# Predicting a reordering of row statistics, scatters, softmax sums and gate rows in an adaLN transformer block

## The reference

```python
mod = (silu(c) @ wmod).reshape(B, 6, 1, -1)
sa, ca, ga, sb, cb, gb = mod[:, 0], ..., mod[:, 5]
h = layernorm(x) * (1 + ca) + sa
x = x + ga * attention(h)          # probs = softmax(causal scores), out = probs @ v @ w_o
h = layernorm(x) * (1 + cb) + sb
x = x + gb * moe(h)                # tok/slot tables, 16 experts, scatter-add, plus shared expert
```

## Time and profile before

| | |
|---|---|
| runs, median (lowest to highest) | 1308.64 us (1308.13 to 1310.06) |
| the profiled execution | 1310.89 us, span 1309.1 us |
| mean granted TensorE clock | 0.95 |
| busy: TensorE matmul / weight load | 87% / 67% |
| busy: VectorE / ScalarE / GpSimd | 65% / 48% / 34% |
| moved by DMA | 114.36 MB, mean 87 GB/s |

### The profile page before, as it was taken

One profiled execution on the slowest core, in us unless ns is written; L12 is line 12 of the kernel. 1 busy time (PEld: TensorE's weight loads), 2 busy tenths in 40 slices (PEclk: granted clock), 3 DMA queues, 4 the chain that ended last, 5 costly groups with the idle time before them and its releaser, 6 DMA issues.

```text
span 1309.1 us, 23512 instructions
## 1 busy us (share of the span) xinstructions
PE 1141.5 (87%) x6444; PEld 882.1 (67%) x6444; DVE 848.4 (65%) x2468; ACT 633.2 (48%) x1840; POOL 439.4 (34%) x460
## 2 busy tenths in 40 slices
PE   6459999998999899998999899998999899998793
PEld 4347777776677677676677677676677677776462
DVE  3447857784687657774688657773788658774641
ACT  2237634565256544564256544564256544663120
POOL 1112104441344305340344305350334315441454
PEclk8779999998999899998999899998999899999897
DMA  9554203530153203530153203530153203430693
GB/s 307 145 129 105 70 1 81 146 84 13 32 145 81 64 1 83 143 93 5 36 145 78 64 1 89 137 97 1 43 144 78 59 0 98 119 91 2 193 255 38
DMA packets 87436, 114.36 MB, mean 87 GB/s; under 512 B 16226, under 2 KB 50976, under 8 KB 87336
## 3 DMA queue, kind: packets, MB, share of 16 engines
q1 hardware_dynamic: 68296, 98.55, 29.2%
q0 software_dynamic: 7168, 6.20, 2.4%
q10 hardware_dynamic: 11872, 8.65, 2.4%
HBM read 35.56 MB, written 15.11 MB: 39 GB/s over the span
## 4 chain that ended last, share of the span: by engine, by line
PE 51%; DVE 17%; issue 11%; DMA 6%; SPq 5%; ACT 4%; POOL 3%; ACTq 2%; DVEq 1%; POOLq 0%
PE PS L780 7%; PE PS L738 5%; PE PS L740 5%; PE PS L739 5%; PE PS L759 4%; SPq L444 4%; PE PS L909 3%; DMA qT<-qstage 3%; PE PS L938 3%; DVE qr L1350 2%; PE PS L888 2%; PE PS L890 2%; DVE pT L1381 2%; PE PS L708 2%; ACT probs L1111 2%
## 5 line engine op out<-in xcount | busy, mean ns | idle before, releaser
L1111 ACT ACTIVATE probs<-probs,nmax 128x512 f32<-128x512 f32 (+3 forms) x512 | 283.2, 554 | 214.5 <-DVE nmax L1364 212.3
L1364 DVE CUSTOM_DVE_ANT_0 probs<-PS,cmask 128x512 f32<-128x512 f32 (+3 forms) x512 | 231.4, 489 | 148.3 <-PE PS L740 121.1
L738 PE MATMUL PS<-kTh,qT 128*128 128x512 f32 (+3 forms) x512 | 182.6, 357 | 62.8 <-DMA qT<-qstage 25.8
L739 PE MATMUL PS<-kTl,qT 128*128 128x512 f32 (+3 forms) x512 | 169.4, 331 | 0.0
L740 PE MATMUL PS<-kTh,qT 128*128 128x512 f32 (+3 forms) x512 | 168.7, 329 | 0.0
L547 POOL TENSOR_TENSOR qr<-qr 128x512 f32<-128x512 f32 x64 | 81.2, 1269 | 257.0 <-DVE qr L1350 256.8
L759 PE MATMUL PS<-ident,probs 128*128 128x128 f32 x1280 | 160.0, 279 | 0.3 <-ACT pT L1120 0.3
L1120 ACT ACTIVATE pT<-PS 128x384 f32<-128x384 f32 (+3 forms) x320 | 125.4, 455 | 69.7 <-PE PS L759 69.2
L780 PE MATMUL PS<-pT,kmat 128*64 128x512 f32 (+3 forms) x1024 | 158.3, 452 | 0.3 <-issue 0.3
L738 PEld LDWEIGHTS PS<-kTh,qT 128*128 128x128 f32 x512 | 99.9, 195 | 86.0 <-issue 32.0
L759 PEld LDWEIGHTS PS<-ident,probs 128*128 128x128 f32 x1280 | 143.6, 143 | 11.6 <-issue 7.7
(11 more groups left out here) (254 smaller groups left out, 1855.7 us busy)
## 6 DMA issues: line engine op xcount, KB each, us to landing
qT<-qstage SPq DMA_DIRECT2D x128, 256.0 KB
qT<-qstage SPq DMA_DIRECT2D x256, 128.0 KB
x_in<-in_x SPq DMA_DIRECT2D x8, 512.0 KB, 6.4
modb<-mod_dram SPq DMA_DIRECT2D x8, 512.0 KB, 6.1
h_dram<-mod_dram SPq DMA_DIRECT2D x1, 4096.0 KB
h_dram<-h SPq DMA_DIRECT2D x8, 512.0 KB, 3.4
out<-base SPq DMA_DIRECT2D x8, 512.0 KB, 4.3
pT<-in_wo SPq DMA_DIRECT2D x1, 2048.0 KB, 11.0
```

Of the source, the lines that this page charges most:

```text
L738: pe.matmul(PS[:, bank, 0:n], qh, kTh[:, 0:n], start=True, stop=False)
L739: pe.matmul(PS[:, bank, 0:n], qh, kTl[:, 0:n], start=False, stop=False)
L1111: act.activation(probs[:, UO[u]:UO[u] + UW[u]], probs[:, UO[u]:UO[u] + UW[u]], ACT.Exp, scale=-1.0, bias=nmax[:, u:u + 1], accum_out=psums ...
L1364: dve.tensor_tensor_reduce(out=probs[:, UO[u]:UO[u] + UW[u]], in0=PS[:, SBANK[u], 0:UW[u]], in1=cmask[:, S - UW[u]:S], scale=-1.0, scalar= ...
```

## The change

Five things are moved.

1. `h1_statistics` is cut in two: bn_stats of tiles 0 and 1 at the end of step 4, of tiles 2 and 3 with all bn_aggr at the end of step 5. `h1_normed` stands in step 6 where the statistics stood.
2. GpSimd's scatters: rounds of three in steps 1 to 4, of four in step 5, none in step 6. The root for h1 is cut out of `roots_pre` and stands behind the last scatter; the wait for the scatters' landing comes after it.
3. `invert_sums` keeps the reciprocal; the spreading copy is GpSimd's (`widen`), between its addition and its subtraction of the query two steps ahead, and alone in steps 6 and 7.
4. `q_low` on VectorE comes behind both `group_out` copies in all steps.
5. The gate rows are written by batch, 512 rows at a time: those of batch 0 after the first three queries, those of batch n after `load_modb(n)`.

Besides, TensorE's latent projection of query 0 in the middle now comes ahead of the wait for h2.

```diff
-            sp.dma_start(h2_dram[0:T, H:].rearrange("(b s) h -> b s h", s=S),
-                         mod_dram[:, 3 * H:].unsqueeze(1).to_broadcast([B, S, H])).then_inc(gates_out, 16)
+            def gate_rows(b):
+                sp.dma_start(h2_dram[bass.ts(b, S), H:].unsqueeze(0),
+                             mod_dram[bass.ds(b, 1), 3 * H:].unsqueeze(1).to_broadcast([1, S, H])).then_inc(gates_out, 16)
...
                 store_batch(b)
                 load_modb(n)
+                gate_rows(n)
...
+            def widen(g):
+                wait_alone(pool, inv_ready, g + 1)
+                pool.tensor_copy(wide[:].rearrange("p (t h d) -> p h t d", t=NT, h=2),
+                                 prec[:].rearrange("p (h t) -> p h t", h=2).unsqueeze(3).to_broadcast(
+                                     [P, 2, NT, KL])).then_inc(wide_ready, 1)
...
-                for j in range(3 * (p - 1), min(3 * p, NT * TOPK)):
+                for j in range(3 * (p - 1), 3 * p if p < NPAIR - 3 else NT * TOPK):
...
                 if pre:
                     pe.wait_ge(kql_ready, 3 * (n + 1))
                     q_rotary(0, n * NPAIR, not post)
+                if pre:
+                    q_latent(0, n * NPAIR, not post)
                 if post:
                     pe.wait_ge(n2_ready, 2 * b + 1)
                     turn_h2()
-                if pre:
-                    q_latent(0, n * NPAIR, not post)
...
                 dve.wait_ge(exp_ready, g * NU + NU)
-                ch.step(dve.reciprocal(prec[:], psums[:]))
-                dve.tensor_copy(wide[:].rearrange("p (t h d) -> p h t d", t=NT, h=2),
-                                prec[:].rearrange("p (h t) -> p h t", h=2).unsqueeze(3).to_broadcast(
-                                    [P, 2, NT, KL])).then_inc(wide_ready, 1)
+                dve.reciprocal(prec[:], psums[:]).then_inc(inv_ready, 1)
...
                 if p == NPAIR - 2 and more:
                     modulation(b + 1)
-                    h1_statistics(b + 1)
+                    h1_normed(b + 1)
...
                 invert_sums(g)
-                if rope and not first:
-                    q_low(g + 2)
                 if not first:
                     values_out(p - 1, g - 1)
                 elif more:
                     gated(b - 1, 1)
                 group_out(g, 3)
-                if rope and first:
+                group_out(g, 5)
+                if rope:
                     q_low(g + 2)
-                group_out(g, 5)
+                if more and p in (NPAIR - 4, NPAIR - 3):
+                    h1_statistics(b + 1, p - NPAIR + 4)
                 if not last:
                     maxima(g + 1, (0, 1, 2))
```

More of the change, by code:

```diff
@@ L52 @@
 HALF = DR // 2
-CHAIN_PROLOGUE, CHAIN_BATCH = 30, 60
+CHAIN_PROLOGUE, CHAIN_BATCH = 29, 52
 MOVES = 6
@@ L311, in adaln_block @@
         exp_ready = sem("exp_ready")
+        inv_ready = sem("inv_ready")
         wide_ready = sem("wide_ready")
@@ L464, in _ @@
             sp.dma_start(h2_dram[T:T + P, H:], zrow[:]).then_inc(gates_out, 16)
-            sp.dma_start(h2_dram[0:T, H:].rearrange("(b s) h -> b s h", s=S),
-                         mod_dram[:, 3 * H:].unsqueeze(1).to_broadcast([B, S, H])).then_inc(gates_out, 16)
+            def gate_rows(b):
+                sp.dma_start(h2_dram[bass.ts(b, S), H:].unsqueeze(0),
+                             mod_dram[bass.ds(b, 1), 3 * H:].unsqueeze(1).to_broadcast([1, S, H])).then_inc(gates_out, 16)
             for p in range(3):
                 move_query(0, p, p < 2)
+            gate_rows(0)
             with sp.Fori(0, B - 1) as b:
@@ L527, in root, with root_h1, roots_kv @@
                 pool.tensor_tensor(dst, dst, mhalf[:, 0:dst.shape[1]], ALU.pow).then_inc(ready, 1)
-            def roots_pre(n):
+            def root_h1(n):
                 wait_alone(pool, var1_ready, NT * (n + 1))
                 root(rstd[:], mv[:, :, 1], LN_EPS, eps1, rs1_ready, n)
+            def roots_kv(n):
                 wait_alone(pool, ssq_ready, 8 * (n + 1))
@@ L542, in roots_post, with query_rotary @@
                 root(rstd2[:, 3:], mv2[:, 3:, 1], LN_EPS, eps2, rs2_ready, 2 * b + 1)
-            def query_rotary(g):
+            def widen(g):
[3 more added lines that the diff above has]
+                                     [P, 2, NT, KL])).then_inc(wide_ready, 1)
+            def query_rotary(g, w=None):
                 wait_alone(pool, turned_ready, g + 1)
                 pool.tensor_tensor(qr[:, 0, :], qr[:, 0, :], qr[:, 1, :], ALU.add).then_inc(rope_ready, 1)
+                if w is not None:
+                    widen(w)
                 wait_alone(pool, peh_ready, g + 1)
@@ L593, in shared @@
                 pool.tensor_tensor(base[:], tmp[:], x1[:], ALU.add).then_inc(base_ready, 1)
-            roots_pre(0)
+            root_h1(0)
+            roots_kv(0)
             pool.wait_ge(x_landed, 16)
@@ L609, in scatter, with between @@
                     ).then_inc(scattered, 16)
[L611 to L615, removed]
+            def between(b, n, more):
+                roots_kv(n)
                 roots_post(b)
@@ L621, in _ @@
                 counts(b, False)
-                query_rotary(n * NPAIR + 2)
+                query_rotary(n * NPAIR + 2, n * NPAIR)
                 shared(b)
-                for p in range(1, NPAIR - 1):
-                    if p + 2 < NPAIR:
-                        query_rotary(n * NPAIR + p + 2)
+                for p in range(1, NPAIR - 2):
+                    query_rotary(n * NPAIR + p + 2, n * NPAIR + p)
                     scatter(b, p)
+                if more:
+                    root_h1(n + 1)
+                widen(n * NPAIR + NPAIR - 2)
+                widen(n * NPAIR + NPAIR - 1)
                 pool.wait_ge(scattered, n * NT * TOPK * 16)
                 pool.sem_inc(entries_free, 1)
+            for p in range(NPAIR):
+                query_rotary(p, p - 2 if p >= 2 else None)
+            root_h1(1)
+            widen(NPAIR - 2)
+            widen(NPAIR - 1)
+            with pool.Fori(0, B - 2) as b:
+                between(b, b + 1, True)
+            between(B - 2, LAST, False)
             roots_post(LAST)
@@ L633, in _ @@
             counts(LAST, True)
-            pool.wait_ge(gates_out, 32)
+            pool.wait_ge(gates_out, 16 * (B + 1))
             pool.wait_ge(tok_ready, 1)
@@ L1302, in _ @@
             dve.tensor_tensor(csl[:], cth[:], cT_sb[:], ALU.mult).then_inc(c_ready, 1)
[L1304 to L1310, removed]
             def normed(src, dst, mean_var, rs, tiles, ready):
@@ L1319, in modulation, with h1_statistics @@
                 dve.tensor_copy(mod1[:], modT[:, 0:4, bass.ds(n, 1)].rearrange("p k b -> p (k b)")).then_inc(mod1_ready, 1)
-            def h1_statistics(n):
+            def h1_statistics(n, half):
                 dve.wait_ge(x_landed, 16 * (n + 1))
-                statistics(x_in, st, mv, var1_ready, range(NT))
+                for t in range(2 * half, 2 * half + 2):
+                    ch.link(dve.bn_stats(st[:, t, :], x_in[:, t, :]))
+                if half:
+                    wait_alone(dve, ch.sem, ch.base + ch.n)
+                    for t in range(NT):
+                        dve.bn_aggr(mv[:, t, :], st[:, t, :]).then_inc(var1_ready, 1)
             def h1_normed(n):
@@ L1406, in step @@
                     part()
-                if p == NPAIR - 2 and more:
-                    h1_normed(b + 1)
                 invert_sums(g)
-                if rope and not first:
-                    q_low(g + 2)
                 if not first:
@@ L1652, in _ @@
             dve.wait_ge(const_ready, 3)
-            h1_statistics(0)
+            h1_statistics(0, 0)
+            h1_statistics(0, 1)
             h1_normed(0)
```

## The result

The changed kernel takes 1275.47 us in the median (1274.24 to 1276.85), the kernel before 1309.27 in the same comparison: a ratio of 0.9736, 95% interval 0.9721 to 0.9752. Faster, as forecast, but outside the range of 1236 to 1272 and 25.5 us above the 1250.

A forecast was written before the change was run, and what follows sets the result against it. TensorE, busy 87%, was taken as the bound, so its standstills counted. Terms -20.0 + 1 - 31.2 - 2.6 - 1.4 - 4.2 = -58.4 from 1310.89 gave 1252.5 profiled, 1250 us median; range 1236 to 1272.

The forecast's parts named there:

- a forecast of 31.2: Step 6, statistics and scatters moved earlier: 4.9 idle and 2.5 low-clock loss gone, 2.1 left; 5.2 us per batch, six times.
- the copy's 0.62: GpSimd's spreading copy of 512 elements: 0.62 us taken, at the one-input copy rate; upper end 1.27.
- the rival from the Trainium skill's GPSIMD Engine Reference (Engine selection): Spreading copy costs GpSimd 1.27, GpSimd being about twice as slow as VectorE: +9 us, 1259; chance 0.15.
- The staging loop: Steps 2 to 5: once-a-step loop through the query staging buffer, low half to low half, binds at 11.85 us; -2.6 over 32 steps.
- The latent projection's 4.2: Middle: projection ahead of the h2 transposes lets feed-forward matmuls start 0.6 us sooner, seven times: -4.2 us (0 to -8).
- the 52.65: Start: query 0's rotary low half ready at 52.6; plus 5.25 for transfers gives first scores at 57.9 instead of 77.93, -20.0 us.
- I take half: 11.85: Steps 2 to 5: loop sum 12.07, rotary transfers up to 0.45 sooner, half taken: 11.85 against 11.94, -2.6 us over 32 steps.
- the stated upper end of 12.07: Steps 2 to 5: staging loop with no transfer gain takes 12.07 us a step, +4 us in all.
- +1 in all; if the cover goes, 7 x 3.8: 512 KB gate-row pieces per batch: 0 to 3.8 us of queue time each; +1 us taken, +27 without cover.
- The rival of held-up queries: 512 KB gate-row pieces hold up query 3 in every batch: +26 us, 1276; chance 0.06.
- The gain in step 0 that I booked at -1.4: Step 0: 0.5 us stall goes, but spreading transposes wait for GpSimd; 0.2 x 7 = -1.4 us (0 to -3.5).
- theory H: e12's expectation: GpSimd's copy delays base addition by 0.45, holding VectorE's seat addition; undone, step 1 shrinks 0.4 to 0.6, 1268 to 1273 us.

The follow-up runs named there:

- e11: Changed kernel with step 6's statistics, root and scatters all back as before, the root behind the last scatter's landing: 1309.19 us, ratio 0.9960.
- e3: Changed kernel with VectorE's low half of the query back at its old place, ahead of the output: 1257.35 us, ratio 0.9572.
- e4: Changed kernel with gate-row pieces behind query 7's transfers and the query's low half at its old place: 1231.94 us, ratio 0.9386.
- e6: e4 with the spreading copy of the inverse sums back on VectorE: 1252.85 us, ratio 0.9543.
- e7: Changed kernel with TensorE's latent projection back behind the transposes of h2: 1283.86 us, ratio 0.9778.
- e12: Changed kernel with GpSimd's base addition ahead of its last rotary subtraction in step 0: 1275.14 us, ratio 0.9699.
- e1: Changed kernel with the gate rows back as one 4 MB write at the start: 1289.51 us, ratio 0.9812.
- e2: Changed kernel with each 512 KB gate-row piece issued after query 7's transfers instead of after modb: 1267.81 us, ratio 0.9659.
- e8: Changed kernel with query 3's transfers issued ahead of output store, modb, gate-row piece and x_in: 1313.26 us, ratio 1.0003.
- e5: e4 with VectorE's loop over the batches written out, so no branch back between steps 0 and 1: 1200.59 us, ratio 0.9135.

## Why the forecast was 25 us short

The 21.7 us between forecast and profiled execution add up, measured less forecast, as: start +2.8, steps 2 to 5 by the loop +8.8, the pieces +7.5, step 1 +7.8, step 6 +2.9, step 0 -2.7, step 7 and the middle -4.9, the end -0.5.

**Right:** the start's mechanism; step 6, at -28.3 in the trace and 31.3 with step 7 in e11 for a forecast of 31.2 (its own terms, 4.9 + 2.5 - 2.1, give 5.3 a batch and not 5.2); the copy's 0.62, which takes 0.610:

```profile
L552 POOL COPY mid<-prec 128x512 f32<-128x512 f32 x64 | 39.0, 610 | 152.8 <-DVE prec L1393 152.8
```

That also settles the rival from the Trainium skill's GPSIMD Engine Reference (Engine selection): unqualified, the rule would have made it 1.27. The staging loop is what is late next, and e3, e4 and e6 show what it hides. One reading was loose: the spreading copy ended 0.29 after GpSimd's addition, not with it. The latent projection's 4.2 measure 0.46 a batch in e7 where the clock stays up, 3.2 in seven.

**Start, +2.8: the 52.65 failed.** It assumed TensorE's prologue unchanged. It is not. Changed kernel:

```profile
42.00:46.00 4.00, 1.88 (x5) 1.49 (x5) 1.51 (x3) 1.18 (x2) 0.00 (x0) 0.50 0.00 0
46.00:50.00 4.00, 4.00 (x13) 2.42 (x13) 2.58 (x4) 0.60 (x1) 1.03 (x1) 0.50 0.00 0
```

The granted clock is 0.50, 1.2 GHz, where the kernel before has 1.00, and GpSimd's subtraction comes at 54.78 instead of 51.31. From its end to the scores are 4.65, not 5.25. In e12 these stretches had 1.00:

```profile
42.00:46.00 4.00, 2.69 (x12) 2.00 (x14) 1.94 (x3) 0.56 (x2) 0.00 (x0) 1.00 0.00 0
```

There the subtraction came at 51.18, and the first scores at 57.10, 0.8 ahead of the forecast. The low clock is no accident of one execution: the other thirteen experiments all have 0.50 from 42 to 46 us, and those with pieces start their scores at 59.5 to 61.0. It is not the pieces' doing either, since e1 has the single write and the low clock. What decides it is open: the idle times ahead of it (3.70, then 2.12) are the same in the kernel before, in e12 and in the changed kernel, and e12's edit stands behind the start.

**Steps 2 to 5: the term "I take half: 11.85" failed in size.** I let the transfers come 0.22 sooner because the rotary ones follow at the issue pitch. They do, but they land no sooner. From the first latent transfer's issue to ScalarE are 534.95 - 527.60 = 7.35, against 578.97 - 571.94 = 7.03, and the issue follows the low half by 0.38 instead of 0.24. So 7.73 stands where I put 7.05; the other terms came out 0.2 shorter. These terms are of one step (batch 3, step 3). With the collisions left aside the mean of steps 2 to 5 is 12.1, about the stated upper end of 12.07: they took 6.2 more instead of 2.6 less.

**Pieces: "+1 in all; if the cover goes, 7 x 3.8" failed in where the cover is.** I looked at the steady batch only. Its cover was VectorE's stop behind the branch, and batches 0 and 7, which have no branch back in step 1, never had it: 8.5 us at once (step 2), 7.8 of which e2 removes. e3, e8 and e12 lay the rest open, in e8 at 3.4 to 6.9 a batch where I had put 3.8 as the upper end. The rival of held-up queries named nearly the measured time, 1276, but by a delay in every batch, which is not what happened.

**Step 1, +9.7 in batches 1 to 6: no term at all.** VectorE's seat addition is held until GpSimd's base addition ends, and I did not look at that pair. The copy does not push the base addition back, as theory H had it: the subtraction ahead of it still waits for ScalarE. First scores of step 0, subtraction and base addition, batch 4, before:

```profile
652.60 0.80 PE L738 MATMUL PS<-kTh,qT 128*128 128x512 f32 x1
667.55 1.30 POOL L549 TENSOR_TENSOR qstage<-qr,qstage 128x512 fp32r<-128x512 f32 x1 [1.22 <-ACT qstage L1106]
668.81 2.40 POOL L593 TENSOR_TENSOR base<-tmp,x 128x1024 f32<-128x1024 f32 x1
```

Changed (the base addition at 640.56 is shown above):

```profile
624.35 0.80 PE L763 MATMUL PS<-kTh,qT 128*128 128x512 f32 x1
639.30 1.30 POOL L563 TENSOR_TENSOR qstage<-qr,qstage 128x512 fp32r<-128x512 f32 x1 [0.66 <-ACT qstage L1131]
```

From the first scores of step 0 to the base addition are 16.21 in both. What moved is TensorE: step 0 is 0.44 shorter (14.83 for 15.27), so step 1 and the seat addition in it come that much sooner, and the base addition ends 3.78 after step 1's first scores instead of 3.34. The gain in step 0 that I booked at -1.4 is what brings the two together. The hold itself stands in the Trainium skill's SBUF — State Buffer (section Who interferes with whom): a VectorE instruction with two SBUF inputs and a GpSimd instruction that reads SBUF exclude each other, and the later one waits. The traces agree: the seat addition takes 0.96 in the changed kernel, 0.51 in e6, where step 0 takes 15.27 again, and 0.24 in e12, with the base addition moved ahead. The stop then lasts 4.1 instead of 3.5, TensorE waits longer, and in four of six batches the mean granted clock of the step falls to 0.81, against 0.90 in the other two. Why the stop itself is 0.6 longer is open. e8 excludes the four transfers; the hold alone is not enough, since e3 has it and stops of 3.51 to 3.88; in e4 the stop ranges from 3.54 to 4.31. Batches 0 and 7 have no branch there, and their step 1 became 0.9 and 1.0 shorter.

**Step 7 and the middle, -9.1 for -4.2**, and step 0, -4.1 for -1.4, went the other way. Of the first, about 3.8 belong to the statistics and scatters (e11) and 3.2 to the latent projection (e7); the other 2.1 are open.

## What to carry to other kernels

Price a transfer in the first and the last pass as well as in the steady one: what covers it may be a stall of another engine, which those passes don't have and the next improvement takes away. When a step gets shorter, look for work on another engine that keeps its place, and for whoever now runs into it: the base addition stood where it was, and VectorE came 0.44 sooner. When two costs hide each other, as the pieces and the stop did, undo them together before judging either (e12 alone gained 0.4%, which is not clear of noise, and the moved pieces alone 0.8%; both gained 2.2%).

## What was unexpected in the hardware

- VectorE's branch back costs 3.1 to 4.3 us of standing still once per batch, and with the low clock behind it step 1 is 4.3 to 5.8 us longer than written out (e4 against e5, six batches): 31.3 us in the median, as much as the largest part of the change (e11).
- A 512 KB copy within device memory, from one row of 1 KB repeated, takes 11.6 us to land, and x_in issued behind it 11.9 instead of 6.4.
- GpSimd's copy with eight runs of 64 equal elements takes 0.610 us, no more than a plain copy's rate gives.
